# An RNN under an LSTM: the first loads in another order, on two queues

## What is computed

```python
def rnn(x, h0, Wx, Wh, b):                    # L0: 512 -> 512, 128 steps
    xW = einsum('ntd,dh->nth', x, Wx) + b
    h = tanh(h @ Wh + xW[:, t])               # step by step

def lstm(x, h0, Wx, Wh, b):                   # L1: 512 -> 4 x 512, 128 steps
    a = einsum('ntd,dg->ntg', x, Wx)[:, t] + b + h @ Wh
    i, f, o, g = sigmoid, sigmoid, sigmoid, tanh of the quarters of a
    c = f * c + i * g;  h = o * tanh(c)

x = x + rnn(x, cond_1024, L0_cond_Wx, L0_cond_Wh, L0_cond_b)      # x: 32 x 128 x 512, float32
x = x + lstm(x, cond_1024, L1_cond_Wx, L1_cond_Wh, L1_cond_b)
```

## Time and profile before

| | us |
|---|---|
| median of three runs | 846.36 |
| lowest, highest | 844.5, 847.37 |
| the profiled execution | 844.77 |
| its span (first to last instruction) | 843.0 |
| PE busy | 827.6 (98%) |
| DVE, ACT, POOL busy | 602.5, 578.9, 289.0 |

### The profile page before, as it was taken

One profiled execution on the slowest core, in us unless ns is written; L12 is line 12 of the kernel. 1 busy time (PEld: TensorE's weight loads), 2 busy tenths in 40 slices (PEclk: granted clock), 3 DMA queues, 4 the chain that ended last, 5 costly groups with the idle time before them and its releaser, 6 DMA issues.

```text
span 843.0 us, 52000 instructions
## 1 busy us (share of the span) xinstructions
PE 827.6 (98%) x22859; PEld 620.9 (74%) x22859; DVE 602.5 (71%) x1722; ACT 578.9 (69%) x1542; POOL 289.0 (34%) x642
## 2 busy tenths in 40 slices
PE   8899999999999999999999999999999999999997
PEld 5555555677787777877778777787777877778896
DVE  3668778877777776777677777668776776767664
ACT  5986476767676667767767776677767767677652
POOL 1312366723323323333332332333333233333320
PEclk9999999999999999999999999999999999999999
DMA  8801100111001111001111000111110000000001
GB/s 309 281 18 27 29 15 16 28 28 26 19 18 30 29 30 29 16 16 30 29 29 29 23 24 17 29 29 30 29 26 20 17 16 17 16 16 16 11 11 28
DMA packets 40195, 30.70 MB, mean 36 GB/s; under 512 B 5772, under 2 KB 38688, under 8 KB 38688
## 3 DMA queue, kind: packets, MB, share of 16 engines
q1 hardware_dynamic: 39712, 27.27, 11.3%
q10 hardware_dynamic: 256, 0.11, 0.0%
HBM read 18.95 MB, written 8.39 MB: 32 GB/s over the span
## 4 chain that ended last, share of the span: by engine, by line
PE 90%; DMA 4%; DVE 3%; ACT 2%; issue 1%; SPq 0%; ACTq 0%; DVEq 0%
PE ps_l L1290 34%; PE ps_l L1356 29%; PE ps_r L1442 9%; PE ps_r L1462 8%; PE ps_l L1334 3%; PE ps_l L1303 2%; PE ps_l L1323 2%; DMA wxl_raw<-in_L_cond_Wx 2%; DMA whl_raw<-in_L_cond_Wh 2%; DMA whr_raw<-in_L_cond_Wh 1%; PE ps_r L1413 1%; PE ps_r L1424 1%; DVE ig L1092 0%; PE ps_l L1277 0%; DVE fc L1090 0%
## 5 line engine op out<-in xcount | busy, mean ns | idle before, releaser
L496 POOL TENSOR_TENSOR xb<-xb,h_l 128x128 f32<-128x128 f32 x127 | 58.2, 458 | 383.8 <-DVE h_lo L1125 379.4
L1090 DVE TENSOR_TENSOR fc<-gates,c 128x128 f32<-128x128 f32 x128 | 39.6, 309 | 150.4 <-ACT gates L780 136.5
L1356 PE MATMUL ps_l<-whl_raw,wxl_raw 128*32 128x256 f16 x3816 | 131.6, 273 | 0.0
L1290 PE MATMUL ps_l<-whl_hi,hT_hi 128*32 128x512 f16 x1888 | 122.5, 379 | 1.1 <-DVE hT_hi L1109 1.1
L1290 PE MATMUL ps_l<-whl_hi,hT_lo 128*32 128x512 f16 x1888 | 122.5, 379 | 0.0
L1290 PE MATMUL ps_l<-whl_lo,hT_hi 128*32 128x512 f16 x1888 | 122.4, 379 | 0.0
L1356 PE MATMUL ps_l<-wxl_hi,wxl_raw 128*32 128x256 f16 x2544 | 115.8, 273 | 0.0
L1356 PEld LDWEIGHTS ps_l<-whl_raw,wxl_raw 128*32 128x32 f16 x3816 | 102.1, 97 | 2.2 <-issue 0.2
L780 ACT ACTIVATE gates<-ps_l,g_products 128x256 f32<-128x256 f32 x114 | 53.5, 469 | 54.2 <-PE ps_l L1290 54.1
L1290 PEld LDWEIGHTS ps_l<-whl_lo,hT_hi 128*32 128x32 f16 x1888 | 51.1, 97 | 50.8
L1290 PEld LDWEIGHTS ps_l<-whl_hi,hT_lo 128*32 128x32 f16 x1888 | 51.1, 97 | 50.8
(11 more groups left out here) (215 smaller groups left out, 1820.6 us busy)
## 6 DMA issues: line engine op xcount, KB each, us to landing
xb<-in_x SPq DMA_DIRECT2D x128, 64.0 KB, 2.2
out<-xb SPq DMA_DIRECT2D x124, 64.0 KB, 1.8
whl_raw<-in_L_cond_Wh SPq DMA_DIRECT2D x4, 1024.0 KB, 6.6
wxl_raw<-in_L_cond_Wx SPq DMA_DIRECT2D x4, 1024.0 KB, 6.0
wxr_raw<-in_L_cond_Wx SPq DMA_DIRECT2D x1, 1024.0 KB, 5.4
whr_raw<-in_L_cond_Wh SPq DMA_DIRECT2D x1, 1024.0 KB, 7.4
out<-xb SPq DMA_DIRECT2D x4, 48.0 KB, 2.2
wxl_raw<-peaks SPq DMA_DIRECT2D x5, 2.0 KB, 2.6
```

The costliest lines, as they stand in the source:

```text
L496: nc.gpsimd.tensor_tensor(xb[g % NX][:, t, :], xb[g % NX][:, t, :], h_l[s % 2][:, :], ALU.add).then_inc(out_done, 1)
L1290: last = nc.tensor.matmul(ps_l[s % 4][quarter(j), :], (hT_hi, hT_lo)[h_part][:, k, :], gate_slice(whl[w_part][k], j), start=False, stop=(h ...
L1356: last = nc.tensor.matmul(at[quarter(j), :], stationary, weights[:, j, :, :], start=False, stop=(y_part == 1 and k == 1), skip_group_check ...
```

## The change

SP issues wxr first, then quarters 2 and 3 of x group 0, then whr. ACT issues quarters 0 and 1 of group 0 behind h0. The RNN bias comes by a transfer with a broadcast source that writes all 128 rows of `bias_r`, in place of PE's product and ACT's copy; ACT copies it from there into the banks of RNN steps 0 and 1 (`r_first_seeded`), for which each bank is first written by a filler. The product of the LSTM bias moves behind the input product of RNN step 0. Groups 3 to 7 of x wait for the last chunk instead of the one before it. Ahead of the first product stand eleven fillers in place of twelve.

```diff
-        def load_x(eng, g):
-            for j, src in enumerate(sliced_dram(x, g * TG)):
+        def load_x(eng, g, quarters=range(J)):
+            for j in quarters:
+                src = sliced_dram(x, g * TG)[j]
                 eng.dma_start(xb[g % NX][quarter(j), :, :], src).then_inc(x_in[g % NX], DMA)
...
-            load_x(sp, 0)
             sp.dma_start(wr_raw[OF_X][:, :], WxR.rearrange("(p k) n -> p (k n)", k=J)).then_inc(s_wr[OF_X], DMA)
+            load_x(sp, 0, (2, 3))
             sp.dma_start(wr_raw[OF_H][:, :], WhR.rearrange("(p k) n -> p (k n)", k=J)).then_inc(s_wr[OF_H], DMA)
...
             load_x(sp, 2)
-            sp.wait_ge(s_wxl[2], DMA)
+            sp.wait_ge(s_wxl[3], DMA)
             load_x(sp, 3)
...
             act.dma_start(h0n[:, :], h0.rearrange("b (j u) -> j b u", j=J)).then_inc(s_h0, DMA)
-            act.dma_start(bias_rows_r, bR.rearrange("(j u) -> j u", j=J)).then_inc(s_bias_r, DMA)
+            load_x(act, 0, (0, 1))
+            act.dma_start(bias_r, bR.rearrange("(j u) -> j u", j=J).unsqueeze(1).broadcast_to([J, B, P])).then_inc(s_bias_r, DMA)
             act.dma_start(bias_rows_l.rearrange("j (g u) -> j g u", g=G),
                           bL.rearrange("(g j u) -> j g u", g=G, j=J)).then_inc(s_bias_l, DMA)
...
-            act.wait_ge(bias_mm, 1)
-            nc.scalar.activation(bias_r, ps_l[2][:, 0:P], ACT.Copy).then_inc(bias_done, 1)
+            act.wait_ge(s_bias_r, DMA)
+            act.wait_ge(r_banks_written, 1)
+            for r in (0, 1):
+                nc.scalar.activation(ps_r[r][:, 0:P], bias_r, ACT.Copy).then_inc(r_first_seeded, 1)
...
                 if t == 0:
                     pe.wait_ge(x_turned, g + 1)
+                if r < 2:
+                    pe.wait_ge(r_first_seeded, r + 1)
...
             pe.wait_ge(ident_done, 1)
+            fill(ps_r[0], 1)
+            fill(ps_r[1], 1).then_inc(r_banks_written, 1)
             fill(ps_l[3], 3)
-            fill(ps_l[0], 2)
+            fill(ps_l[0], 3)
             fill(ps_end, 1)
-            pe.wait_ge(spread_j_done, 1)
-            pe.wait_ge(s_bias_r, DMA)
-            nc.tensor.matmul(ps_l[2][:, 0:P], spread_j, bias_rows_r, start=True, stop=True).then_inc(bias_mm, 1)
-
-            for r in (0, 1):
-                nc.tensor.matmul(ps_r[r][:, 0:P], spread_j, bias_rows_r, start=True, stop=True)
-            pe.wait_ge(s_bias_l, DMA)
-            nc.tensor.matmul(ps_l[1][:, :], spread_j, bias_rows_l, start=True, stop=True).then_inc(bias_mm, 1)
-            pe.wait_ge(bias_done, 1)
-            fill(ps_l[2], 6).then_inc(banks_written, 1)
+            fill(ps_l[2], 2).then_inc(banks_written, 1)
             product_r(0)
...
                 if k == 0:
+                    pe.wait_ge(spread_j_done, 1)
+                    pe.wait_ge(s_bias_l, DMA)
+                    nc.tensor.matmul(ps_l[1][:, :], spread_j, bias_rows_l, start=True, stop=True).then_inc(bias_mm, 1)
                     fill(ps_pk, 2)
```

## The result

| | before | after |
|---|---|---|
| median | 845.55 us (844.5 to 847.37, 5 runs) | 851.35 us (851.29 to 851.87, 5 runs) |
| ratio, 95% interval | | 1.0066 [1.0052, 1.008] |
| the profiled execution | 844.77 us | 851.3 us |
| its span | 843.0 us | 849.5 us |

The change makes the kernel 5.8 us slower (851.35 less 845.55), where 5.7 was forecast, and 851.35 lies in the forecast's own range of 850 to 855. It comes out right partly by luck. The biases were put too late and the slack of ACT too low, which made the loss too large; PE's products were put too short, which made it too small; and the step from ACT to PE at its end was wrong.

What follows compares the result with a forecast made beforehand. Weight loads bound the kernel to 37 us, then PE, with ACT's chain nearly as tight. Late x and biases add 5.7 to 844.77, giving 850.5; the median's 1.6 makes 852.1 us. Range 843.5 to 855.0, the forecast's own 850 to 855.

Steps and rivals of the forecast that it cites:

- the slack of ACT: ACT's chain from the first RNN tanh to its first LSTM gates: 0.7 us to spare in the whole stretch.
- From ACT to PE: LSTM start: late gates delay PE's recurrent product of step 1 and input product of step 3, the latter to 54.4, 5.7 later.
- ACT's queue starves beside 8 KB packets: DMA at the start: each short row on ACT's queue waits out a 0.31 us chunk packet; x at about 14.0 against 4.89.
- one and one: DMA engine sharing: an engine alternates between two queues, one whole packet from each per turn; a 25 ns row costs 0.31 us.
- x on ACT's queue, the term that decides: Two quarters of x on ACT's queue: x and biases late, first tanh 19.05 instead of 11.78, kernel 5.7 us later.
- PE's first products: RNN step 0: product 0 0.87 us (1.08 with pipeline), LSTM bias product 1.02, two fillers; recurrent product 0 at 17.9.
- WhR 1.0 earlier: Weight loads: issuing WxR and two x quarters ahead lands WhR up to 1.0 us earlier, or 0 if x rows eat it.
- the last chunk 1.4 earlier: Last weight chunk: x groups 3 to 7 moved behind it give 1.4 us, between 0 and 2.3.
- By bytes: Rival on DMA sharing: short rows are not held, x and biases in by about 6; 844.3 us; chance 0.22.
- Whole transfers: Rival on DMA sharing: a queue keeps an engine for all rows of one transfer; 847.7 us; chance 0.12.
- No earlier start: Rival: loads do not start earlier, WhR and last chunk held as before; 846.4 us, no difference; chance 0.06.

Runs made afterwards that it cites:

- e2: The change, with SP issuing WhR only when both biases have landed, so ACT's queue has the engines to itself behind WxR: 846.75 us, ratio 1.002.
- e6: The change without its new load order and x groups, leaving the broadcast RNN bias and its PE and ACT parts: 849.37 us, ratio 1.0051.
- e9: The change, with ACT's four transfers in the order LSTM bias, RNN bias, h0, x: 852.41 us, ratio 1.0092.
- e7: The change, with all of x group 0 on SP behind WxR and none on ACT's queue: 849.93 us, ratio 1.0059.
- e5: The kernel before, with WxR as SP's first transfer and all of x group 0 behind it, ahead of WhR: 848.35 us, ratio 1.0041.
- e4: The change, with 38 more fillers ahead of product 0 to keep PE busy in its wait: 849.46 us, ratio 1.0047.
- e10: e5 with one change: ACT issues the two biases (4 and 16 rows) ahead of h0: 844.4 us, ratio 1.0002.
- e1: The change, with the RNN bias as before (4 rows, PE's products, ACT's copy) and LSTM bias product ahead of product 0: 850.54 us, ratio 1.0063.
- e3: The kernel before, with only x groups 3 to 7 waiting for the last chunk instead of the one before: 844.4 us, ratio 1.0.
- e11: e10 plus x groups 3 to 7 behind the last chunk: 844.95 us, ratio 1.0.
- e12: e11 with six more fillers ahead of the bias products: 845.01 us, ratio 1.0004.
- e13: The kernel before, with sixteen more fillers between product 0 and recurrent product 0: 848.23 us, ratio 1.0039.

## Why the prediction came out as it did

**ACT's queue starves beside 8 KB packets: right.** e2 shows it by taking the packets away, e6 by adding 124 rows to an untouched order of loads, e9 by changing who is last. The arrangement is not one and one, though. Where WxR is issued first, nothing of ACT's queue but what had started ahead of it is served while it streams (none from 2.0 to 4.5 us in the change); beside short rows ACT's pass almost freely; beside later chunks 1.2 rows go with each packet from 9 to 12 us, and many more from 12.5 to 13.5. The 113 rows that passed from 5.0 to 5.5 fit x at 11.5 instead of 14.0, and the 120 packets from 12.5 to 13.5 the biases at 14.4 to 14.6 instead of 15.5 to 15.7. The Trainium skill (DMA: Bandwidth & Descriptors, Queues, rings and completion order) has an engine drain a packet of typically 9 to 17 descriptors before it switches. In the change WxR with its eight rows and a completion on each engine went through in one piece, which agrees; the rows that pass beside WxR in e6 (49 packets from 5 to 10 us) and the 42 rows beside 36 chunk packets from 9 to 12 us don't.

**"x on ACT's queue, the term that decides": half of it.** The prediction counted x's turns with the biases', and its chain waited for the bias, but it named x. e7 has no x on ACT's queue, and its step 3 is still 3.4 us late (52.11 less 48.68), where the change's is 6.6 late. e5 (WxR first) and e6 (broadcast bias) lose 0.41% and 0.51% alone. They don't add up, because each does the same: a small transfer that PE waits for is issued after, or is too long to end before, 8 KB packets fill the engines.

**PE's first products: under-sized.** The working had the old durations behind a wait of PE that it had itself forecast: 0.87 + 1.02 + fillers + 1.08. With 9.26 us of idle time ahead of them they ran at the lower level, and the first tanh came at 21.68 instead of 19.05 although its bias was 1.1 earlier. From the bias to the tanh it had 3.55 us and 7.29 were measured (21.68 less 14.39). e4 divides the difference: from the start of product 0 to the tanh it takes 3.74 us at the full clock (18.66 less 14.92), the change 6.84 and the prediction 3.27, so 3.1 us are the clock, 0.5 the products and fillers, and the rest is ahead of product 0.

**From ACT to PE: the step that failed.** The prediction said that PE waits twice, for h ahead of the recurrent product of LSTM step 1 and for `y_scale` ahead of the input product of step 3, which would start 9.39 behind the gates. The trace has neither wait: from 35.44 to 55.26 PE is busy for 19.82 of 19.82 us, the input product of step 3 starts at 55.26, and `y_scale` (L637) ends at 56.5, behind it; its result is for LSTM steps 4 and 5. What holds PE is ACT's pass over the last WhL chunk, which ends at 35.40; from there PE runs through in 19.8 us. In the change, e5, e6, e7 and e9 the distance from the first tanh to step 3 is 33.58, 33.58, 33.59, 33.57 and 33.67 us. In e10, whose first tanh comes at 14.13 and in which ACT holds PE too, it is 33.77. So ACT's chain reaches 48.68 with a first tanh at 15.1 (48.68 less 33.6): **by this working ACT had 3.3 us to spare** behind its first tanh at 11.78, where the prediction gave it 1.6 (0.7 ahead of the gates and 0.9 ahead of step 3). Put together: the tanh is 9.9 late, 3.3 of that is free, 6.6 remain, and step 3 is 6.6 late. The prediction had 7.3, 0.7 and 0.9 off, and 5.7. It had three quarters of the delay and half of the slack, and the errors met. Its last step was luck too: it added the 1.6 us by which the median of three runs of the kernel before lay above the profiled execution (846.36 less 844.77). The change has no such distance (851.35 and 851.3), so 850.5 and 1.6 stand against an execution of 851.3.

The span follows step 3 by 794.1 to 794.6 us in before, the change, e1, e2, e3, e4, e9, e11, e12 and e13, and by 794.6 to 796.0 in e5, e6, e7 and e10. In these four the extra time lies behind the last tanh of the RNN: 37.7 to 39.0 us to the end, against 37.3 in before and in the change. Waits of PE on "issue" are 1.3 us of it in e7, 0.3 in e5 and 0.2 in e6; e10 has none. With a first tanh ahead of 15.1 (e3, e10, e12) the time doesn't move.

**WhR 1.0 earlier and the last chunk 1.4 earlier: neither came.** WhR was issued 1.0 earlier and landed 0.26 later. On 12 engines its rows were in by 9.82; on the four that carry ACT's rows between 10.38 and 10.85. That bound, 0 "if the x rows eat it", was the right end. The x groups gave 0.4 alone (e3), and in the change the last chunk landed 1.4 later than before. It costs nothing, as PE was by then held by ACT.

**The rivals.** By bytes (844.3): rows were held, so no. Whole transfers (847.7): it fits WxR alone, where WxR is issued first. No earlier start (846.4): the first tanh is 9.9 later.

**Open.** Why nothing of ACT's queue is served during WxR, while e9's 16 rows were served with WxR's first packets: whether issue time decides it or the first packets' own slowness (0.8 us in the mean) was not separated. What let 120 packets pass from 12.5 to 13.5 us was not tried either. And what brings PE's waits on "issue" in some executions (e2 to e4, e7, e11 to e13) was not tried; they follow packets of instructions.

No version tried beats the kernel before: the best, e3, e10, e11 and e12, have ratios of 1.0 to 1.0004.

## What to carry to other kernels

A small transfer that an engine waits for has to be issued ahead of the first large one, on whatever queue: e10 and e5 differ by the place of one line on ACT's queue and by 3.9 us in their medians (848.35 less 844.4). Replacing work of an engine that is idle anyway by a transfer is a loss when the transfer has 128 rows and the DMA engines are full; 4 rows and a product were cheaper. And slack is not the idle time in a window: follow the engine's chain to the instruction where another engine really takes its result, and look there which of the two comes last.

## What the runs showed of the hardware

- A row of 512 B takes 27 ns when an engine serves it, but on four engines beside 8 KB packets some 0.3 us passed for each row from 9 to 12 us in the change. A 64 KB broadcast load took 11.54 us from issue to landing.
- A queue with two kinds of transfers, short rows and 8 KB rows, changes how fast the other queue moves: 115 packets in 0.5 us beside short rows, 50 in 3 us beside chunks. The turn is not a fixed one: beside chunks too, 120 passed from 12.5 to 13.5 us.
- PE's clock was at its 1.2 GHz level after idle times of 9.26 us (the change, 0.50 granted) and 6.41 (e6, product 0 in 1.93 us). Fillers through the wait kept it at 2.4 (e4).
- At the start of every profiled execution PE works at the lower level: one filler starts 0.43 us behind the other, and 0.22 in e4's long row of them. The trace's record of the clock begins with its first rise, at 4.65 us in before, and a view prints 1.00 ahead of it. In e1, e5, e9, e10, e11 and e13 that first entry comes at 19.98, 15.80, 24.56, 12.15, 13.44 and 11.99 us. So in e9 the products from 15.4 to 22.2 us took 1.94 and 2.07 us at a printed 1.00; ahead of the first entry the durations tell the level. e13 has the instructions of before up to there, so the first rise can come at another time for the same work.

```profile
15.40:22.20 6.80, 6.77 (x75) 3.93 (x79) 2.68 (x3) 0.00 (x0) 0.00 (x0) 1.00 1.05 333
```
